# A transformer kernel on one core whose engine programs are ordered anew inside each round

## What is computed

```python
def _layer(x, wqkv, qs, ksc, wo, lg, lb, w1, b1, w2, b2):
    h = shift_token(x)                       # half of the columns one row down
    q, k, v = split(h @ wqkv)                # 128 -> 3 x 512
    q, k = l2norm(q) * qs, l2norm(k) * ksc
    q, k = rotary_xpos(q, k)                 # cos and sin tables with a scale
    x = x + local_attention(q, k, v) @ wo    # 64 queries see 128 keys
    h = layernorm(shift_token(x)) * lg + lb
    a, g = split(h @ w1 + b1)                # 341 + 341
    return x + (a * gelu(g)) @ w2 + b2

x = x + 0.5 * stack(layernorm(x))            # stack: two such layers
x = x + attention(layernorm(x))              # causal, 1024 rows, one head of 128
x = x + 0.5 * stack(layernorm(x))
```

## Time and profile before

| | us |
|---|---|
| median of 3 runs | 2624.45 |
| lowest and highest run | 2623.68, 2626.21 |
| span of the profiled execution, its own time | 2623.2 |
| busy: TensorE | 2558.0 (98%) |
| busy: VectorE | 2376.0 (91%) |
| busy: ScalarE | 2346.8 (89%) |
| busy: GpSimd | 2056.4 (78%) |

### The profile page before, as it was taken

The page is one execution under the profiler, slowest core; times in us unless marked ns, Lnnn a source line. Parts: engine busy times, 40 slices in busy tenths (PEclk is TensorE's granted clock), DMA queues, the critical chain, the costliest instruction groups (busy, mean ns, idle before and its releaser), DMA issues.

```text
span 2623.2 us, 80275 instructions
## 1 busy us (share of the span) xinstructions
PE 2558.0 (98%) x29132; PEld 2063.6 (79%) x29132; DVE 2376.0 (91%) x6206; ACT 2346.8 (89%) x7379; POOL 2056.4 (78%) x2185
## 2 busy tenths in 40 slices
PE   5999999999999999998999999999999999999998
PEld 4778777877788888886997777778777788888876
DVE  7999999999999999996888999999998999999995
ACT  5999999999999999995555999999999999999996
POOL 7999999988887877872104999999988888787873
PEclk8999999999999999999999999999999999999999
DMA  4121111111111111110000111111111111111110
GB/s 105 44 51 31 28 38 31 28 28 39 24 32 28 28 42 26 32 28 8 9 1 11 32 28 32 26 38 32 29 24 39 28 32 40 30 40 36 36 40 26
DMA packets 63810, 83.95 MB, mean 32 GB/s; under 512 B 11538, under 2 KB 30652, under 8 KB 63420
## 3 DMA queue, kind: packets, MB, share of 16 engines
q1 hardware_dynamic: 63420, 78.82, 13.1%
HBM read 11.67 MB, written 4.19 MB: 6 GB/s over the span
## 4 chain that ended last, share of the span: by engine, by line
PE 83%; POOL 6%; DVE 5%; ACT 4%; issue 2%; SPq 0%; DMA 0%; ACTq 0%; POOLq 0%; DVEq 0%
PE PS L678 8%; PE PS L662 8%; PE PS L628 7%; PE PS L652 7%; PE PS L619 6%; PE PS L742 6%; PE PS L621 6%; PE PS L620 6%; PE PS L723 4%; PE PS L725 3%; PE PS L724 3%; PE PS L644 3%; PE PS L690 2%; PE PS L853 2%; PE PS L692 2%
## 5 line engine op out<-in xcount | busy, mean ns | idle before, releaser
L4440 ACT ACTIVATE P<-PS,MX 128x128 f32<-128x128 f32 x2048 | 754.3, 430 | 2.1 <-DVE MX L2248 1.2
L5756 POOL TENSOR_TENSOR T<-T,SQ 128x512 f32<-128x512 f32 x512 | 652.1, 1284 | 115.3 <-DVE SQ L2209 111.7
L5792 POOL TENSOR_TENSOR P<-P,RI 128x512 f32<-128x512 f32 x512 | 527.8, 1042 | 73.8 <-DVE RI L2254 71.7
L4440 ACT ACTIVATION_READ_ACCUMULATOR P<-PS,MX 128x1 f32 x2048 | 535.6, 268 | 0.0
L5769 POOL TENSOR_TENSOR T<-T,RN 128x512 f32<-128x512 f32 x512 | 525.9, 1048 | 6.2 <-DVE RN L2242 3.8
L2190 DVE TENSOR_REDUCE SS<-SQ 128x8 f32<-128x512 f32 x512 | 343.8, 681 | 44.6 <-ACT SQ L4395 37.9
L4395 ACT ACTIVATE SQ<-PS 128x512 f32<-128x512 f32 x512 | 338.1, 662 | 45.9 <-PE PS L621 35.0
L619 PE MATMUL PS<-WH,YH 128*128 128x512 f32 x768 | 346.1, 451 | 6.9 <-POOL YL L5745 3.3
L2248 DVE TENSOR_REDUCE MX<-PS 128x4 f32<-128x512 f32 x512 | 345.8, 678 | 6.5 <-PE PS L652 6.3
L2209 DVE TENSOR_TENSOR SQ<-PS,TAB 128x512 f32<-128x512 f32 x512 | 349.1, 682 | 2.3
L2201 DVE TENSOR_TENSOR T<-PS,TAB 128x512 f32<-128x512 f32 x512 | 344.2, 682 | 7.1 <-PE PS L628 3.3
(11 more groups left out here) (155 smaller groups left out, 5938.4 us busy)
## 6 DMA issues: line engine op xcount, KB each, us to landing
VP<-VP SPq DMA_DIRECT2D x480, 128.0 KB, 2.3
out_dram<-X SPq DMA_DIRECT2D x16, 256.0 KB, 2.6
X<-in_L_attn_x_dram SPq DMA_DIRECT2D x7, 512.0 KB, 4.5
SG<-in_L_ffn_w_dram SPq DMA_DIRECT2D x5, 341.0 KB, 3.0
SG<-in_L_ffn_wqkv_dram SPq DMA_DIRECT2D x4, 384.0 KB, 3.4
SGQ<-in_L_ffn_wqkv_dram SPq DMA_DIRECT2D x4, 256.0 KB, 3.5
X<-in_table_dram SPq DMA_DIRECT2D x2, 512.0 KB, 6.5
P<-in_L_ffn_wo_dram SPq DMA_DIRECT2D x2, 256.0 KB, 3.2
```

Of the source, the lines that this page charges most:

```text
L4440: ins = act.activation(P[:, g, p, :], PS[:, b, 128 * p:128 * p + 128], ACT.Exp, bias=MX[:, g, p:p + 1], accum_out=SM[:, g, p:p + 1])
L5756: pool.tensor_tensor(T1[:, k, :], T1[:, k, :], SQ[:, (2 * n + 1 - x) % 3, :], ALU.add).then_inc(added[x], 1)
L5792: pool.tensor_tensor(P[:, g], P[:, g], RI[:, g, :].unsqueeze(2).broadcast_to([128, NPAIR, 128]), ALU.mult).then_inc(p_scaled, 1)
```

## The change

No function computes anything else, and each engine has the same instructions (TensorE the same 20383 matmuls); what changes is their order and with it some waits. The loop's body is cut at another place, so ROUNDS has other bounds and all lags other numbers, which by itself moves nothing. The tables of the PSUM banks follow: ROTA keeps the same users in each bank. A steady round has the same tiles under way as before.

```diff
-ROUNDS = {0: (9, 32), 1: (41, 63)}
+ROUNDS = {0: (4, 32), 1: (36, 64)}
 ROTA = [
-    [("W2", 4), ("TK1", 3), ("O0", 4), ("V1", 2), ("TK0", 2), ("S0", 2), ("P2", 3), ("G0", 3)],
+    [("O0", 4), ("V1", 2), ("TK0", 2), ("S0", 2), ("P2", 3), ("G0", 3), ("W2", 3), ("TK1", 1)],
```

The weight casts of layers 1 and 3 leave the functions that called them on the side (split_y, square, rotate_add, normalise_qk) and get calls of their own in the loops of ScalarE and GpSimd:

```diff
+        def stage_qk(u):
+            if 2 * u in (NCH, 3 * NCH):
+                for part in (0, 1):
+                    stage_wa(layer_of_pair(u), part)
```

More of the change, by code:

```diff
@@ L1365, in into_attention @@
             a_turn_p(0, 0, 0)
+            turn_y(PAIRS - 1)
             a_turn(0, 1)
@@ new lines, in local @@
+                root(t - 1, 4)
+                row_max(t - 2, 2)
+                root(t - 1, 5)
+                root(t - 1, 6)
+                root(t - 1, 7)
+                root(t - 1, 8)
+                y1_low(s - 2)
+                root(t - 1, 9)
+                y1_high(s - 2)
+                gate(s - 3, 0)
+                gate(s - 3, 1)
+                row_max(t - 2, 3)
+                gate(s - 3, 2)
+                sum_squares(t, 0, Q)
+                row_inverse(t - 2, 2)
+                sum_squares(t, 0, K)
@@ L3140, in into_attention, with attention @@
+                y0_up(t + 1)
+                rotate_cos(t, 0, Q)
+                rotate_sin(t, 0, K)
+                y_next(s - 3)
+                rotate_cos(t, 0, K)
+                row_inverse(t - 2, 3)
+                rotate_sin(t, 0, Q)
+                sum_squares(t, 1, K)
+                rotate_cos(t, 1, K)
+                row_max(t - 1, 0)
+                rotate_sin(t, 1, K)
+        def attention():
+            row_max(TURN - 3, 1)
+            a_stats(0, 0)
             rows_stats(PAIRS - 3)
-            row_max(TURN - 3, 1)
+            x_next(PAIRS - 4)
@@ L4384, in split_y @@
             act.copy(YH[:, n % 3, :], Y0[:, col:col + 128]).then_inc(y_hi, 1)
-            if t in (NCH, 3 * NCH) and i == 1:
-                for part in (2, 3):
-                    stage_wa(layer(t), part)
         def square(t, i, x):
@@ L4395, in square @@
             act.activation(SQ[:, m % 3, :], PS[:, bank_of("QK"[x] + str(i), t), :], ACT.Square).then_inc(squared[x], 1)
-            if t in (NCH - 1, 3 * NCH - 1) and i == 1 and x == Q:
-                for part in (0, 1):
-                    stage_wa(layer(t) + 1, part)
         def copy_k(t, i):
@@ L4565, in a_copy_far @@
             act.copy(PTF[i % 4][:, 512:512 + n], PS[:, A_TURN[1], 0:n]).then_inc(a_pcB, 1)
+        for n in range(4):
+            stage_wa(0, n)
         def first_steps():
@@ L4585, in first_steps @@
             copy_k(0, 0)
+            square(1, 1, K)
+            copy_k(0, 1)
             square(1, 1, Q)
-            square(1, 1, K)
+            copy_q(0, 1)
+            exp_rows(0, 0)
+            exp_rows(0, 1)
             y0_down(2)
@@ new lines, in local @@
+                exp_rows(t - 3, 0)
+                square(t - 2, 1, Q)
+                exp_rows(t - 3, 1)
+                split_o(t - 4, 0)
+                split_o(t - 4, 1)
+                split_y(t - 1, 1)
+                copy_v(t - 2, 0)
+                norm_rows(s - 3)
+                copy_v(t - 2, 1)
+                square(t - 1, 0, K)
+                copy_p(t - 3, 0)
+                exp_rows(t - 3, 2)
+                copy_q(t - 2, 0)
+                square(t - 1, 0, Q)
+                copy_k(t - 2, 0)
@@ new lines, in local @@
+                copy_k(t - 2, 1)
+                split_hn(s - 3)
+                square(t - 1, 1, K)
+                exp_rows(t - 3, 3)
+                exp_rows(t - 2, 0)
+                copy_p(t - 3, 1)
+                copy_q(t - 2, 1)
+                copy_p(t - 3, 2)
+                copy_p(t - 3, 3)
+                square(t - 1, 1, Q)
+                stage_qk(s)
+                exp_rows(t - 2, 1)
+                split_o(t - 3, 0)
+                copy_v(t - 1, 0)
+                split_o(t - 3, 1)
@@ new lines, in local @@
+                y0_down(t)
+                gelu(s - 3, 0)
+                split_y(t, 0)
+                gelu(s - 3, 1)
+                split_y(t, 1)
+                gelu(s - 3, 2)
+                round_w1(s - 2)
+                exp_rows(t - 2, 2)
+                square(t, 0, Q)
+                square(t, 0, K)
+                copy_q(t - 1, 0)
+                exp_rows(t - 2, 3)
+                copy_v(t - 1, 1)
+                stage_v(s)
+                y0_down(t + 1)
+                copy_k(t - 1, 0)
@@ L5012, in into_attention, with attention @@
+                copy_p(t - 2, 0)
+                square(t, 1, K)
+                split_y(t + 1, 0)
+                copy_p(t - 2, 1)
+                copy_k(t - 1, 1)
+                copy_p(t - 2, 2)
+                copy_q(t - 1, 1)
+                copy_p(t - 2, 3)
+        def attention():
             exp_rows(TURN - 3, 0)
             square(TURN - 2, 1, Q)
-            copy_q(TURN - 3, 1)
             exp_rows(TURN - 3, 1)
@@ L5348, in out_of_attention @@
             copy_p(TURN + 4, 1)
+            copy_k(TURN + 5, 1)
             copy_p(TURN + 4, 2)
+            copy_q(TURN + 5, 1)
             copy_p(TURN + 4, 3)
[L5351 to L5360 removed]
@@ L5756, in rotate_add @@
             pool.tensor_tensor(T1[:, k, :], T1[:, k, :], SQ[:, (2 * n + 1 - x) % 3, :], ALU.add).then_inc(added[x], 1)
-            if t in (NCH - 1, 3 * NCH - 1) and i == 0 and x == Q:
-                for part in (0, 1):
-                    stage_wa(layer(t) + 1, part)
         def normalise_qk(t, i, x):
```

4628 lines of the change are left out of this document (1169 added, 3459 removed), and 173 rows, old and new, of tables (FIRST_USERS, LAST_USERS, ROTA).

## The result

The changed kernel takes 2665.66 us (median of 4 runs, 2662.66 to 2666.72) against 2624.13 us: ratio 1.0154, interval 1.0140 to 1.0168. It is 41.5 us slower. The forecast was 2621.5 and the range ended at 2634, so neither the value nor the range held. The profiled execution took 2662.66 us with a span of 2660.9.

What follows compares the result with a forecast made beforehand. TensorE was taken as the bound, busy 2558 of 2623 us, so rounds and transitions decide. Begin +2, into the attention −3, out of it −2, rounds and end 0 gave −3: span 2620.2, median 2621.5 us; range 2609 to 2634.

Steps and rivals of the forecast that it cites:

- The steady round: Loop rounds: four terms summing to +0.04 us per round, taken as nothing; bounds −5 to +5 over 52 rounds.
- −0.48: Steady round, ScalarE: copy_q leaves the tight stretch by running before the last copy_p, saving 0.48 us per round.
- +0.47: Steady round, TensorE: turn_q goes ahead of the turn_p that starts the stretch, adding 0.44 to 0.50 us.
- The stall of 0.12: Steady round, ScalarE: exp_rows' late start goes because row_max now stands ahead of the reciprocal, saving 0.12 us.
- The weight casts: Layers 1 and 3: casts gathered in one place of one round, twice in the kernel; nothing, −1 to +1 us.
- The begin: Kernel start: statistics ahead of the root delay it 4 us, partly caught up; +2 us, bounds 0 and +6.
- Into the attention: Way into the attention: first-batch attention work fills a third of TensorE's holes; −3 us, bounds −6 and +1.
- Out of the attention: Way out of the attention: the wait for GpSimd's y_lo goes; −2 us, bounds −4 and +1.
- A: Rival: the steady round shortens by −5 to −16 us beside the −3, 2605 to 2617; chance 0.25.
- B: Rival: a tile's last exponentials come late and delay turn_p in the rounds, +10 us, 2632; chance 0.20.
- C: Rival: the begin costs the full +6 us and the transitions give −0 to −2, 2628 to 2631; chance 0.15.
- D: Rival: same matmuls bound the rounds and idle time only moves; 2624, within the forecast's chance of 0.40.

Runs made afterwards that it cites:

- after: The changed kernel itself, all engines' lists in the new order, against the kernel before the change: 2665.7 us, ratio 1.0154.
- b_tab: The changed kernel with only VectorE's products for the second layer's tables moved earlier, behind ln_eps(7): 2662.6 us, ratio 1.0152.
- begin_old: The changed kernel with the calls of first_steps on all four engines back in the old order: 2652.5 us, ratio 1.0103.
- out_early_old: The changed kernel with only the stretch from the middle of the attention to scored131 (tile 65's first scores) in old order: 2665.6 us, ratio 1.0164.
- out_old: The changed kernel with the calls from the middle of the attention to the second loop in old order: 2657.1 us, ratio 1.0134.
- w1_late: The changed kernel with round_w1 back behind the round's second split_y on ScalarE and rest_of_w1 a round later on GpSimd: 2667.1 us, ratio 1.0161.

## Why the prediction was wrong

**The steady round** was right in size: forecast 0 within ±5, measured +0.08 in layers 0 and 2 and −0.01 in 1 and 3, together 1.2 us. Two of its four terms were not as told. ScalarE at the start of that loop, of after, against the earlier trace rows:

```profile
472.96 0.59 ACT L2999 COPY QT<-PS 128x512 f32<-128x512 f32 x1 [0.95 <-PE PS L561]
473.44 0.60 ACT L3027 COPY PT<-PS 128x512 f32<-128x512 f32 x1
```

copy_q did not leave the stretch: it waits 0.95 us for turn_q and now opens it. From there to the turn_p at 489.18 it is 16.22 us, before 16.25 from 459.55 to 475.80. So the −0.48 and the +0.47 were both nothing, and the 0.08 lies in the other piece of the round, from that turn_p to the next such copy: 20.69 us (to 509.87) against 20.58 (to 496.38). The stall of 0.12 did go, and ScalarE's lag did stay (the exp_rows that releases that turn_p takes 1.68 instead of 1.48), as forecast.

**The weight casts**, "taken as nothing, −1 to +1": failed, 5.7 us in after's trace, 4.2 of it without the lower clock. I looked at the casts of wqkv that were gathered, and not at round_w1, which moved twelve calls up in ScalarE's round and stands, twice in the kernel, behind a wait for TensorE. A step that runs twice in 64 rounds looks like no step in a round of the other 62.

**The begin**: the first part was right within 2 us (root 33.6 forecast, 32.4 measured; turn_q1 34.8 and 34.1; turn_k1 38.2 and 37.1; turn_q3 near 50, measured 51.4). The step that failed is the one behind it, "+3, and about 1 more is caught up behind it: +2". Nothing was caught up. scored3 came 7.5 late, the tables' products, which now stood behind two waits, holding some 3 to 4 of it (b_tab), and the ramp made 13.4 of it, in other executions 17 to 19. The clock's share is at least the 4 us by which scored3 to scored7 differs between executions of the same begin. The Trainium skill's rule that was weighed ("TensorE: Matmul & The Clock Gate", section "What's actually happening": the throttled clock is the default, activity releases it) pointed the right way. These traces agree in part: the granted clock fell behind waits of TensorE, but behind the same wait of 1.82 us in the round of w1 it fell in after (0.79) and not in begin_old (1.00).

**Into the attention**: −3 forecast, +2.6 measured. The wait of 1.69 ahead of the blocks of w1 is gone; those of 1.61 and 1.74 ahead of it stand, and one of 1.45 for a gate has come:

```profile
1234.94 0.66 PE L699 MATMUL PS<-CST,G 128*128 128x128 f32 x4 [1.61 <-DVE G L1761]
1237.33 0.41 PE L723 MATMUL PS<-CST,T 128*128 128x128 f32 x2 [1.74 <-ACT G L3049]
1247.19 0.22 PE L758 MATMUL PS<-MCAU,IDB 128*128 128x128 bf16 x1 [1.45 <-DVE G L1743]
```

The first attention work brought in (L723, a_turn_w) didn't run in the hole: it takes PSUM bank 1, which YR held before, and so waits 1.74 us for norm_rows (L3049), a step of the chain. That this is why nothing was won is argued from these rows, not shown. TensorE idles 11.9 us from the 29th down to the first product with v, before 10.1. With the old middle 1.0 is left of the 2.6; no run takes the way in alone.

**Out of the attention**: −2 forecast, +13.8 measured, the largest error. The expected wait went, and its place was taken by the root, between whose steps two rotations now run (its last step starts at 1451.4 us against 1428.5 before, 2.2 more than the 20.8 by which the attention was late), by the lower clock in the same stretch (0.83 against 1.00), and by the ramp. In the sum's own terms: the −2 for y_lo looked at one wait, and the ramp behind it had no term.

**The rivals**: A and B, to which 0.45 went, did not happen. C named the begin and the right sign with too small a price, 6 for a measured 13.4, because the bound came from the clock alone, and it had the way out at −2 to 0, where 13.8 were lost. D had the round right and the time wrong. The error common to all terms is that I read each transition up to its next scores, and priced the rounds between there and the loop, 70 us in the begin and as many behind the attention, at nothing, though their order was new on all four engines. In after's trace they hold 5.9 and 7.8 of 37.7 us of lateness.

Open: what in the ramp costs. It is shown that its order does (out_early_old against out_old, 8.3 and 0.9 from scored131 to the 34th down); two attempts to name one chain failed, each moving the wait to the next engine. Also open are the last 0.08 us of the round, and how much of the begin and of the way out is the clock's.

## What to carry to other kernels

When lists of several engines are reordered at once, compare the start of one marker per round in both traces before looking at any wait: the steps of lateness give the place of each loss. A transition is not over with its first busy stretch; count the half-filled rounds until the loop has its steady length, and every step with a wait that only some rounds run. Moving one call forward pays only if the other engines' lists want it in that order too: here both repairs of the ramp made it longer, 8.9 and 9.1 us instead of 7.8.

## What the runs showed of the hardware

Six kernels with the same program up to the second down differed by up to 5.6 us at it (13.4 to 19.0 late). The granted clock goes with it: in after TensorE was at 1.2 GHz from 50 to 60 us, ahead of its wait for VectorE, and at 2.4 GHz for nearly all of the stretch behind it; in w1_late it was at 2.4 GHz for most of the first stretch and at 1.2 GHz for most of the second, and the step behind the wait took 4.0 us more, since the dense work comes there. The full clock ahead of the wait won nothing: scored3 came at 63.3 instead of 62.2.

The same holds for one wait in a dense loop. Behind a wait of 1.82 us in the round of w1 the granted clock was 0.79 over 8 us in after and 1.00 in begin_old, and the round cost 3.6 or 2.1 us by it. Twelve other kernels with that round fall on one of these two sides, so a single execution doesn't tell what such a wait costs.
